# Layer 3's attention: float32r scores from two row halves, readings and row sums between the pairs

## Chip, cores and metric

The kernel runs on one core of a Trainium2 chip (trn2). The metric is the device time of one execution in microseconds (us), taken as the median of several. Lower is better.

## The reference, cut to what matters

The kernel computes four transformer-like layers on x (64 batches of 64 tokens, 256 features). The change is in the attention of layer 3, eight heads over a context `ctx_2048` of the same shape:

```python
def _L3_xattn_ref(q, k, v, gamma):
    ...
    qh = q.reshape(B, h, dq, Lq)
    kh = k.reshape(B, h, dq, Lk)
    vh = v.reshape(B, h, dv, Lk)
    scale = 1.0 / jnp.sqrt(jnp.asarray(dq, dtype=q.dtype))
    qk = jnp.einsum('bhdq,bhdl->bhql', qh, kh) * scale
    sm = jax.nn.softmax(qk, axis=-1)
    ret = jnp.einsum('bhql,bhdl->bhdq', sm, vh)
    return gamma * ret.reshape(B, Dv, Lq)
x = x + _L3_xattn_ref(_layernorm(x, axis=-1), ctx_2048, ctx_2048, L3_xattn_gamma)
```

The 64 tokens of a batch play the part of the channels: a head has 8 of them, and the 256 features are the positions. So there are 64 x 8 score matrices of 256 x 256, each a product over only 8 channels, in float32 accuracy.

## The kernel before, in words

**Tiles, quads, units.** Two batches make a tile of 128 rows; there are 32 tiles. A tile has 16 (batch, head) pairs, called units, in four quads i of four units r. Tiles run in order, written out for the first and last four and as a loop over groups of four between.

**Operands.** Products in float32 accuracy are made from bfloat16 parts. The context, as keys, is split into three parts by GpSimd (POOL) in layer 0's attention (`split`, L355 to L359) and stored to `k_parts` in device memory. The normalized x, as queries, is split into three parts during layer 3's attention, four tiles ahead (`AHEAD`): VectorE (DVE) normalizes (L230), ScalarE (ACT) copies the high part (`high`, L2807) and the middle one (`mid`, L2814), POOL makes the rest and the low part (`rest_and_low`, L2678, L2682). SyncE (SP) stores them (`store`, L2590), waits until they have landed, and loads q and k for four tiles ahead of the one just finished (`load`, L2598, L2601, L2605): 9 products of parts x 8 channels = 72 rows (`ROWS3`), 4 KB per row and batch. The first four tiles are loaded in the stage before (ternary). Rows 72 and 73 of q hold the negated row maxima, against ones in k.

**Two passes of scores.** For each unit TensorE (PE) first makes the scores with queries on partitions (`score`, L2722: two matmuls, 72 rows, 256 columns), two tiles ahead (`LEAD`). DVE takes their maxima, negated (`maxima`, L2855). POOL splits the 128 x 32 maxima of a tile in two bfloat16 parts (`split_max`, L2658, L2660), PE transposes them (`turn_max`, L2733), ACT copies them to `rows` (`rows_copy`, L2800), and SP lays them into rows 72 and 73 of q (`lay_rows`, L2612). In the second pass PE makes the scores turned, keys on partitions, with 74 rows, so that the maximum is already taken off (`score_turned`, L2742), and ACT takes the exponential (`exponent`, L2825).

**Reading.** `read` multiplies a quad's exponentials with the values (L2759) and with ones, for the row sums (L2765). Each matmul there uses a strip of 32 columns of the array, four strips side by side; float32 matmuls run as two instructions, so the records count twice as many as the code. For the quads in `SUMMED` (0 to 2) POOL has added up the two halves of the keys before (`add_lengths`, L2668), and the row sums take 4 matmuls, otherwise 8. ACT copies the tile's output and row sums away (`out_copy`, L2819, L2820), DVE inverts the sums (L2861), POOL multiplies and adds to x (`finish`, L2689, L2691).

**Order.** Each engine's order is written out by hand. PE, per quad i of tile a: for r in 0 to 3 a score of tile a+2 and a turned score of tile a; then the reading of quad i-1. The transpose for tile a+1 stands before quad 2. ACT: four exponentials per quad; the output copies of tile a-1 stand behind exponential (1, 0), the rows' copy before quad 2, `high` behind (2, 3), `mid` behind quad 3. POOL: `split_max` in quad 0, values in quad 1, `finish` of tile a-1 behind (2, 3), `rest_and_low` in quad 3. DVE: the reciprocal behind maximum (2, 0). SP, per tile: rows, stores, loads.

**Banks.** Scores use banks 0 to 3, one per unit; turned scores banks 4, 5, 7 and again 4, so that unit 3 must wait for the exponential of unit 0 of its quad and unit 0 for that of unit 3 of the quad before (`turned_after`); the output is in bank 6; the transposed maxima in bank 3.

```python
turned_bank, turned_after = (4, 5, 7, 4), (1, 4, 4, 3)
...
pe.wait_ge(s["exp_ready"], unit_ready(a.t, i, r) - turned_after[r])
...
if i == 0:
    pe.wait_ge(s["val_ready"], tile_ready(a.t))
    pe.wait_ge(s["out_copied"], tile_ready(a.t) - 1)
```

The last wait holds the first reading of a tile until the output of the tile before is copied out.

## Time and profile before

| what | value |
|---|---|
| median of 3 executions | 2258.29 us (2255.62 to 2261.69) |
| the profiled execution | 2276.26 us |
| its span in the trace | 2274.0 us |
| PE, weight loads, DVE, ACT, POOL busy over the span | 84%, 64%, 70%, 44%, 49% |
| layer 3's attention, first score to last reading | about 1420 to 1908 us |
| granted clock of PE in 1460 to 1880 | 1.00 |

The profile is of one execution. Busy shares are over all stages, and a stage has its own limit. Matmuls are pipelined, and the ends of their records are modelled, so what PE spends on one is read from the distance between starts, not from its duration. A number behind an arrow in brackets in a row is idle time of the engine before it, and what ended it.

### The profile page before, as it was taken

Reading aid. Unit: us, or ns where it says so; the run is one execution under the profiler, and the core shown is the slowest. Engines: PE = TensorE matmul, PEld = TensorE weight load, DVE = VectorE, ACT = ScalarE, POOL = GpSimd, SP = SyncE. Lnnn points to the kernel's source line nnn. Section 1 sums busy time; section 2 is a strip of 40 time slices with the busy share of each in tenths; the row PEclk is TensorE's granted clock in tenths of the full one; section 3 lists DMA queues with packets and bytes.
Section 4 is the critical chain, followed back from the end, with each engine's and each line's share of the span. In section 5 each row is a group of like instructions: output and inputs, shape, how many; then the busy total and the mean of one; then the engine's idle time right before and its main releaser. Section 6 shows DMA issues by size and latency. Waiting matters only on the chain. (4 is left out here: it accounts for less than half of the span.)

```text
span 2274.0 us, 46815 instructions
## 1 busy us (share of the span) xinstructions
PE 1915.3 (84%) x15870; PEld 1457.1 (64%) x15870; DVE 1592.3 (70%) x3825; ACT 995.0 (44%) x2486; POOL 1115.9 (49%) x1467
## 2 busy tenths in 40 slices
PE   6979845398885988898887897899999998879993
PEld 5869612387664777777776787466666664547772
DVE  7865732469668889898886665888888785443446
ACT  3733221134233455554443332466666665423330
POOL 4630026524365666666663100488888775643331
PEclk8989857699997999999998999799999999989996
DMA  7631036600240000000000210144444433223337
GB/s 211 230 102 54 10 117 175 186 20 6 63 128 26 1 0 0 0 0 0 0 0 11 69 39 1 31 109 109 109 108 109 106 86 88 88 94 96 106 108 238
DMA packets 140384, 172.62 MB, mean 76 GB/s; under 512 B 31410, under 2 KB 121698, under 8 KB 135586
## 3 DMA queue, kind: packets, MB, share of 16 engines
q1 hardware_dynamic: 130385, 148.01, 23.7%
q0 software_dynamic: 9808, 22.23, 3.3%
q8 instruction: 101, 1.65, 0.3%
q14 instruction: 90, 0.73, 0.1%
HBM read 117.59 MB, written 52.00 MB: 75 GB/s over the span
## 5 line engine op out<-in xcount | busy, mean ns | idle before, releaser
L2855 DVE TENSOR_REDUCE mx<-bank 128x2 f32<-128x512 f32 x512 | 321.0, 678 | 77.9 <-PE bank L2722 77.2
L2825 ACT ACTIVATE e<-bank 128x512 f32<-128x512 f32 x512 | 269.1, 606 | 135.3 <-PE bank L2742 135.3
L2668 POOL TENSOR_TENSOR es<-e 128x256 f32<-128x256 f32 x384 | 271.7, 730 | 90.5 <-ACT e L2825 90.0
L1915 POOL TENSOR_TENSOR q_l<-q_l,rot_l 64x512 f32<-64x512 f32 x128 | 162.3, 1268 | 131.0 <-DVE rot_l L2113 131.0
L2722 PE MATMUL bank<-k,q 72*128 72x256 bf16 x1024 | 203.6, 284 | 15.7 <-DMA k<-k_parts 7.5
L2742 PE MATMUL bank<-q,k 74*128 74x256 bf16 x1024 | 195.5, 274 | 5.9 <-DMA q<-rows 3.8
L2759 PE MATMUL bank<-e,val 128*32 128x256 f32 x2048 | 138.8, 388 | 3.1 <-ACT nd L2820 0.7
L2722 PEld LDWEIGHTS bank<-k,q 72*128 72x128 bf16 x1024 | 92.0, 100 | 76.5 <-issue 24.5
L3040 POOL DMA_INDIRECT y<-y,y_row x71 | 69.2, 975 | 128.4 <-DVE y L3315 123.5
L1947 PE MATMUL bank<-qcT,wq_abs 96*128 96x128 f32 x1024 | 127.4, 285 | 0.0
L1947 PEld LDWEIGHTS bank<-qcT,wq_abs 96*128 96x128 f32 x1024 | 121.5, 198 | 2.5
L1972 PE MATMUL bank<-wvo,rd_l 128*128 128x256 f32 x512 | 116.4, 381 | 0.0
L2742 PEld LDWEIGHTS bank<-q,k 74*128 74x128 bf16 x1024 | 97.5, 98 | 29.2 <-DMA q<-rows 8.6
L3300 DVE TENSOR_TENSOR hid<-bank,sig 128x176 f32<-128x176 f32 x103 | 35.0, 340 | 113.8 <-issue 45.0
L3173 ACT ACTIVATE sig<-bank 128x176 f32<-128x176 f32 x103 | 32.7, 318 | 176.2 <-PE bank L3096 152.9
L1984 PE MATMUL bank<-key_l,q_l 128*64 128x64 f32 x2048 | 75.5, 227 | 40.6 <-POOL q_l L1915 40.6
L2043 ACT ACTIVATE sc_l<-sc_l 128x512 f32<-128x512 f32 x64 | 40.4, 631 | 156.7 <-POOL sc_l L1901 156.7
L1972 PEld LDWEIGHTS bank<-wvo,rd_l 128*128 128x128 f32 x512 | 95.3, 191 | 16.4 <-ACT rd_l L2055 0.4
L1984 PEld LDWEIGHTS bank<-key_l,q_l 128*64 128x64 f32 x2048 | 66.2, 140 | 55.9 <-POOL q_l L1915 42.0
L975 POOL DMA_INDIRECT xg<-xn_rows,slot_idx x16 | 16.1, 1008 | 170.0 <-POOLq L555 165.4
L2111 DVE TENSOR_TENSOR q_l<-bank,const_sb 64x512 f32<-64x512 f32 x128 | 88.9, 694 | 14.9 <-PE bank L1947 10.9
L3096 PE MATMUL bank<-w,xT 128*128 x284 | 98.1, 468 | 0.2 <-issue 0.2
(455 smaller groups left out, 5031.4 us busy)
## 6 DMA issues: line engine op xcount, KB each, us to landing
k<-k_parts SPq DMA_DIRECT2D x96, 192.0 KB
q<-q_parts SPq DMA_DIRECT2D x32, 576.0 KB
got<-rows SPq DMA_DIRECT2D x71, 129.0 KB
moe_rows<-zero_a SPq DMA_DIRECT2D x16, 512.0 KB
w<-in_e0w SPq DMA_DIRECT2D x16, 512.0 KB
parts_y<-y SPq DMA_DIRECT2D x32, 256.0 KB
k_parts<-k_parts_a SPq DMA_DIRECT2D x96, 64.0 KB, 2.1
q_parts<-parts SPq DMA_DIRECT2D x96, 64.0 KB, 2.0
```

The source lines that it names most:

```text
L1915: nc.gpsimd.tensor_tensor(q[64:P, j, four(m), :], q[64:P, j, four(m), :], rot[64:P, j, four(m), :], ALU.add).then_inc(s["rope_added"], 1)
L1947: last = nc.tensor.matmul(bank(j, h // 4)[:, (h % 4) * P:(h % 4 + 1) * P], wq[:, h, :], qcT[:, j, :], start=True, stop=True)
L1972: last = nc.tensor.matmul(bank(j, 2)[:, 0:D], rd[:, j, hp, :], wvo[:, hp, :], start=(hp == 0), stop=(hp == HP - 1))
L1984: last = nc.tensor.matmul(bank(j, h // 8)[r, (h % 8) * S:(h % 8 + 1) * S], q[:, j, h, r], key[:, j, r], start=True, stop=True)
L2111: v.tensor_tensor(q[64:P, j, four(m), :], raw[64:P], tab(c.cos, 64, P), ALU.mult)
L2668: nc.gpsimd.tensor_tensor(es[:, n, :], e[:, n, 0, :], e[:, n, 1, :], ALU.add).then_inc(s["sum_ready"], 1)
L2722: last = nc.tensor.matmul(scores(r)[:, qt * D:(qt + 1) * D], q[0:R, b, h * D + qt * P:h * D + qt * P + P], k[0:R, b, h * D:(h + 1) * D], s ...
L2742: last = nc.tensor.matmul(scoresT(r)[:, lt * D:(lt + 1) * D], k[:, b, h * D + lt * P:h * D + lt * P + P], q[:, b, h * D:(h + 1) * D], star ...
L2759: nc.tensor.matmul(readout[32 * r:32 * r + 32, 0:D], val[:, a.n % 2, r, i, lt, :], e[:, slot(i, r), lt, :], start=(i == 0 and lt == 0), st ...
L2825: nc.scalar.activation(e[:, slot(i, r), :, :].rearrange("p k n -> p (k n)"), scoresT(r)[:, :], ACT.Exp).then_inc(s["exp_ready"], 1)
L2855: v.tensor_reduce(mx[:, a.n, 0, at:at + 2], scores(r)[:, :].rearrange("p (a n) -> p a n", a=2), AX.X, ALU.max, negate=True).then_inc(s["ma ...
L3096: last = nc.tensor.matmul(gates(u)[:, 0:2 * HID3], src(k), w(k), start=(k == 0), stop=(k == DK - 1))
```

## The change

The parts become two float32r ones (a rounded high part and the rest) instead of three bfloat16 ones, for keys and queries: 4 products x 8 channels = 32 rows per head (`ROWS3`). Heads are put in two halves of the partitions, 0 to 63 and 64 to 127 (`BASE3`): units r = 0 and 2 in one, 1 and 3 in the other. Within a half, rows 32 to 61 are zero in q and one in k and stay so, and rows 62 and 63 hold the negated maxima against ones; the first pass uses 62 rows, the second all 64. PE issues units in pairs (`score_pair`, `turned_pair`), alternating between the halves, each into its own bank. Per quad it now issues turned pair 0, score pair 0, the reading (`read`), turned pair 1, score pair 1, the row sums (`read_lengths`). POOL adds up the keys for quads 0 and 1 only. The transposed maxima go to bank 7. The middle parts and their copies are gone (`mid`), `x_low` is one subtraction on POOL that waits for ACT's `high`. q and k of a tile come by four DMAs each instead of one and three, the rows by two.

```diff
 HH3 = HID3 // 2
-BUF3, ROWS3 = 4, 9 * DQ3
+BUF3, ROWS3 = 4, 4 * DQ3
+BASE3, TOP_ROW3 = (0, P // 2), P // 2 - 2
...
             def split(t):
-                parts, rest, src = k_parts[:, t % KR, :, :], k_rest[:, t % KR, :], ctx_in[:, t % CTX, :]
+                parts, src = k_parts[:, t % KR, :, :], ctx_in[:, t % CTX, :]
                 pool.wait_ge(s[ctx_loaded[t % CTX]], 32 * (t // CTX) + 32)
-                wait(pool, k_stored[t % KR], 48 * (t // KR))
-                nc.gpsimd.tensor_copy(parts[:, 0, :], upper(src))
-                nc.gpsimd.tensor_tensor(rest, src, upper(src), ALU.subtract).then_inc(s["a_split"], 1)
+                wait(pool, k_stored[t % KR], 32 * (t // KR))
+                nc.gpsimd.tensor_copy(parts[:, 0, :], src).then_inc(s["a_split"], 1)
                 pool.wait_ge(s["a_split"], t + 1)
-                nc.gpsimd.tensor_copy(parts[:, 1, :], upper(rest))
-                nc.gpsimd.tensor_tensor(parts[:, 2, :], rest, upper(rest), ALU.subtract).then_inc(s["k_low_ready"], 1)
...
+                for n, (a, value) in enumerate(((c.k3, 1.0), (c.q3, 0.0))):
+                    for m, base in enumerate(BASE3):
+                        at = slice(base + ROWS3, base + 2 * ROWS3)
+                        nc.gpsimd.memset(whole(a[at, t, :]), value).then_inc(s["p_keys"], 1)
+                        pool.wait_ge(s["p_keys"], 4 * t + 2 * n + m + 1)
 
             def step(t, j):
                 pool.wait_ge(s["xlow_ready"], ready(t))
                 if t < 2 * BUF3:
-                    nc.gpsimd.memset(c.k3[64:ROWS3 + 2, t, :].bitcast(F32), ONES).then_inc(s["p_keys"], 1)
...
+def head_rows(ap, both, g):
+
+    return ap[:, :, 2 * H3 * both:2 * H3 * both + 2 * H3, :].rearrange("a c (b g h) l -> g (a c) b (h l)", b=2, g=2)[g]
+
+
+def copied_rows(ap, both, g, b):
+
+    return head_rows(ap, both, g)[:, b, :].unsqueeze(1).broadcast_to([2 * DQ3, 2, H3 // 2 * D])
...
-        SUMMED = range(0, QU - 1)
+        SUMMED = range(0, QU - 2)
...
-        max_rows = c.bank[3][0:8 * H3, 0:P]
+        max_rows = c.bank[7][0:8 * H3, 0:P]
...
-                cols, both = bass.ds(2 * a.t * H3, 2 * H3), slice(2 * a.n, 2 * a.n + 2)
-                q_rows = c.q_parts[:, :, cols, :].rearrange("a c h l -> (a c) (h l)").unsqueeze(1)
-                sp.dma_start(q[0:R, both, :], q_rows.broadcast_to([3 * DQ3, 3, 2 * H3 * D])).then_inc(s[qk_loaded[a.n]], 16)
-                k_rows = c.k_parts[:, :, cols, :].rearrange("c m h l -> (c m) (h l)")
-                for m in range(3):
-                    sp.dma_start(k[3 * DQ3 * m:3 * DQ3 * (m + 1), both, :], k_rows).then_inc(s[qk_loaded[a.n]], 16)
+                both = slice(2 * a.n, 2 * a.n + 2)
+                for g, base in enumerate(BASE3):
+                    for b in range(2):
+                        sp.dma_start(whole(q[base:base + R, 2 * a.n + b, :]),
+                                     copied_rows(c.q_parts, a.t, g, b)).then_inc(s[qk_loaded[a.n]], 16)
+                    for m in range(2):
+                        sp.dma_start(whole(k[base + 2 * DQ3 * m:base + 2 * DQ3 * (m + 1), both, :]),
...
-                sp.dma_start(q[R:R + 2, 2 * a.n:2 * a.n + 2, :], rows[:, a.n, :]).then_inc(s[rows_loaded[a.n]], 16)
+                for g, base in enumerate(BASE3):
+                    at = slice(base + TOP_ROW3, base + TOP_ROW3 + 2)
+                    sp.dma_start(whole(q[at, 2 * a.n:2 * a.n + 2, :]),
+                                 whole(rows[4 * H3 * g:4 * H3 * g + 4 * H3, a.n, :])).then_inc(s[rows_loaded[a.n]], 16)
...
+            def x_low(a):
                 b = a.n % 2
-                wait(pool, "xq_ready", a.t + 1)
-                wait(pool, "mid_ready", a.t - 1)
-                wait(pool, "low_ready", a.t)
+                wait(pool, "high_ready", a.t + 1)
                 if a.exists(-2):
-                    pool.wait_ge(s[stored[b]], 48 * uses(a))
+                    pool.wait_ge(s[stored[b]], 32 * uses(a))
                 settle(pool, s["pool_passed"])
-                nc.gpsimd.tensor_tensor(rest[:, b, :], xq[:, b, :], upper(xq[:, b, :]),
-                                        ALU.subtract).then_inc(s["rest_ready"], 1)
-                wait(pool, "rest_ready", a.t + 1)
-                settle(pool, s["pool_passed"])
-                nc.gpsimd.tensor_tensor(parts[:, b, 2, :], rest[:, b, :], upper(rest[:, b, :]),
+                nc.gpsimd.tensor_tensor(parts[:, b, 1, :], xq[:, b, :], whole(parts[:, b, 0, :]),
                                         ALU.subtract).then_inc(s["low_ready"], 1)
...
-            def score(a, i, r, turned=None):
-                if i == 0 and r == 0:
-                    pe.wait_ge(s[qk_loaded[a.n]], 64 * a.g + 64)
-                pe.wait_ge(s["max_ready"], unit_ready(a.t, i, r) - NP1)
-                if turned is not None:
-                    pe.wait_ge(s["rows_ready"], tile_ready(turned.t))
-                b, h = batch_head(a.n, i, r)
+            def score_pair(a, i, p):
+                if i == 0 and p == 0:
+                    pe.wait_ge(s[qk_loaded[a.n]], 128 * a.g + 128)
+                pe.wait_ge(s["max_ready"], unit_ready(a.t, i, 2 * p + 1) - NP1)
                 for qt in range(2):
-                    last = nc.tensor.matmul(scores(r)[:, qt * D:(qt + 1) * D],
-                                            q[0:R, b, h * D + qt * P:h * D + qt * P + P],
-                                            k[0:R, b, h * D:(h + 1) * D], start=True, stop=True)
-                last.then_inc(s["scores_ready"], 1)
-
-            def turn_max(a):
-                if a.exists(1):
-                    pe.wait_ge(s["max_ready"], unit_ready(a.t + 1, 1, 3))
+                    for r in (2 * p, 2 * p + 1):
+                        base, b, at = place(a.n, i, r)
+                        last = nc.tensor.matmul(scores(r)[:, qt * D:(qt + 1) * D],
+                                                q[base:base + TOP_ROW3, b, at + qt * P:at + qt * P + P],
+                                                k[base:base + TOP_ROW3, b, at:at + D], start=True, stop=True)
+                        if qt == 1:
+                            last.then_inc(s["scores_ready"], 1)
+
+            def turn_max(a, freed_at):
+                pe.wait_ge(s["exp_ready"], freed_at)
...
-            def score_turned(a, i, r):
-                if i == 0 and r == 0:
-                    pe.wait_ge(s[rows_loaded[a.n]], 16 * a.g + 16)
-                pe.wait_ge(s["exp_ready"], unit_ready(a.t, i, r) - turned_after[r])
-                b, h = batch_head(a.n, i, r)
+            def turned_pair(a, i, p):
+                if i == 0 and p == 0:
+                    pe.wait_ge(s[rows_loaded[a.n]], 32 * a.g + 32)
+                pe.wait_ge(s["exp_ready"], max(unit_ready(a.t, i, r) - turned_after[r] for r in (2 * p, 2 * p + 1)))
                 for lt in range(DK):
-                    last = nc.tensor.matmul(scoresT(r)[:, lt * D:(lt + 1) * D],
-                                            k[:, b, h * D + lt * P:h * D + lt * P + P],
-                                            q[:, b, h * D:(h + 1) * D], start=True, stop=True)
-                last.then_inc(s["turned_ready"], 1)
+                    for r in (2 * p, 2 * p + 1):
+                        base, b, at = place(a.n, i, r)
+                        used = slice(base, base + TOP_ROW3 + 2)
+                        last = nc.tensor.matmul(scoresT(r)[:, lt * D:(lt + 1) * D], k[used, b, at + lt * P:at + lt * P + P],
+                                                q[used, b, at:at + D], start=True, stop=True)
+                        if lt == DK - 1:
+                            last.then_inc(s["turned_ready"], 1)
 
             def read(a, i):
 
-
-                if i in SUMMED:
-                    pe.wait_ge(s["sum_ready"], 4 * (len(SUMMED) * a.t + i + 1) + 16)
-                else:
-                    pe.wait_ge(s["exp_ready"], unit_ready(a.t, i, 3))
+                pe.wait_ge(s["exp_ready"], unit_ready(a.t, i, 3))
...
+            def read_lengths(a, i):
+
+                if i in SUMMED:
+                    pe.wait_ge(s["sum_ready"], 4 * (len(SUMMED) * a.t + i + 1) + 16)
...
                     turning = i == 2 and a.exists(1)
                     if turning:
-                        turn_max(a.to(1))
-                    for r in range(4):
+                        turn_max(a.to(1), unit_ready(a.t, 1, 2))
+                    for p, part in enumerate((read, read_lengths)):
+                        if turning and p == 1:
+                            pe.wait_ge(s["rows_ready"], tile_ready(a.t + 1))
+                        turned_pair(a, i, p)
                         if a.exists(LEAD):
-                            score(a.to(LEAD), i, r, a.to(1) if turning and r == 3 else None)
-                        score_turned(a, i, r)
-                    if i > 0:
-                        read(a, i - 1)
-                    elif a.exists(-1):
-                        read(a.to(-1), QU - 1)
+                            score_pair(a.to(LEAD), i, p)
+                        if i > 0:
+                            part(a, i - 1)
+                        elif a.exists(-1):
+                            part(a.to(-1), QU - 1)
```

`mid` and the middle part are taken out of ACT's program in the same way here and in the ternary stage, and semaphore counts follow.

PE's order, with the names of the operands (`k,q` a score, `q,k` a turned score, `e,val` a reading, `ones` row sums). Before, quad 3 of the first tile, with the reading of quad 2:

```order
L2722 MATMUL bank<-k,q 128x256 x2
L2742 MATMUL bank<-q,k 128x256 x2
L2722 MATMUL bank<-k,q 128x256 x2
L2742 MATMUL bank<-q,k 128x256 x2
L2722 MATMUL bank<-k,q 128x256 x2
L2742 MATMUL bank<-q,k 128x256 x2
L2722 MATMUL bank<-k,q 128x256 x2
L2742 MATMUL bank<-q,k 128x256 x2
L2759 MATMUL bank<-e,val 32x256 x8
L2765 MATMUL bank<-es,ones 32x256 x4
```

Every score and turned score alternate unit by unit, and the reading with its row sums stands behind all eight pairs of matmuls. The same place with the change:

```order
L2746 MATMUL bank<-q,k 128x256 x4
L2724 MATMUL bank<-k,q 128x256 x4
L2759 MATMUL bank<-e,val 32x256 x8
L2746 MATMUL bank<-q,k 128x256 x4
L2724 MATMUL bank<-k,q 128x256 x4
L2770 MATMUL bank<-e,ones 32x256 x8
```

A reading now stands after the first two turned and the first two scored units, and the row sums after the other two: between one turned pair and the next there are 4 score matmuls and 8 (or 4) narrow ones.

## Rows read from the trace of the kernel before

**Rows 1.** The view of one line, L2733: the transpose, PE.

```profile
L2733 PE MATMUL bank<-const_sb,mx x30: 298/300/300, 1454.2 to 1874.3; 128*64 128x128 f32 x30
```

**Rows 2.** Timeline of PE (start us, us, engine line op operands, count), two quads.

```profile
1650.26 1.05 PE L2765 MATMUL bank<-e,ones 128*32 128x256 f32 x16
1651.23 0.39 PE L2722 MATMUL bank<-k,q 72*128 72x256 bf16 x2
...
1654.82 0.39 PE L2722 MATMUL bank<-k,q 72*128 72x256 bf16 x2
...
1656.37 0.38 PE L2742 MATMUL bank<-q,k 74*128 74x256 bf16 x2
1656.68 1.07 PE L2759 MATMUL bank<-e,val 128*32 128x256 f32 x16
1657.56 0.61 PE L2765 MATMUL bank<-es,ones 128*32 128x256 f32 x8
1658.11 0.39 PE L2722 MATMUL bank<-k,q 72*128 72x256 bf16 x2
```

**Rows 3.** Waits of PE in 1460 to 1880 (us, times, longest).

```profile
PE bank L2722 <- DMA k<-k_parts: 7.5, 11, 1.7
PE bank L2742 <- DMA q<-rows: 3.8, 14, 0.4
```

**Rows 4.** Timeline of PE in the ternary stage: float32r, 256 columns.

```profile
1343.97 0.28 PE L2337 MATMUL bank<-w_t,hhigh_t 128*128 128x256 f32 x1
1344.20 0.28 PE L2337 MATMUL bank<-w_t,hhigh_t 128*128 128x256 f32 x1
```

**Rows 5.** Timeline of weight loads, two 64-column halves in turn, layer 2.

```profile
903.43 1.48 PEld L1984 LDWEIGHTS bank<-key_l,q_l 128*64 128x64 f32 x48 [0.33 <-issue]
```

**Rows 6.** Timeline at the stage's end, where no scores are left.

```profile
1884.72 0.60 ACT L2825 ACTIVATE e<-bank 128x512 f32<-128x512 f32 x1 [1.20 <-PE bank L2742]
...
1885.57 0.37 ACT L2820 COPY nd<-bank 128x256 f32<-128x256 f32 x1
...
1886.09 1.07 PE L2759 MATMUL bank<-e,val 128*32 128x256 f32 x16 [0.33 <-ACT nd L2820]
...
1890.48 0.83 PE L2742 MATMUL bank<-q,k 74*128 74x256 bf16 x6
1890.91 2.07 ACT L2825 ACTIVATE e<-bank 128x512 f32<-128x512 f32 x4 [0.77 <-PE bank L2742]
1891.56 0.11 PEld L2742 LDWEIGHTS bank<-q,k 74*128 74x128 bf16 x2 [0.53 <-ACT e L2825]
```

**Rows 7.** Timeline of DVE in quad 2: the reciprocal and the maxima after it.

```profile
1655.85 1.74 DVE L2861 RECIPROCAL rec<-nd 128x256 f32<-128x256 f32 x1
...
1657.51 4.21 DVE L2855 TENSOR_REDUCE mx<-bank 128x2 f32<-128x512 f32 x7
```

**Rows 8.** The first load's issue, and a window after it (last: DMA share, GB/s).

```profile
1650.37 0.87 SPq L2598 DMA_DIRECT2D q<-q_parts  x1
...
1660.00:1661.00 1.00, 1.00 (x21) 0.65 (x24) 1.00 (x2) 0.83 (x2) 1.00 (x2) 1.00 0.02 5
```

**Rows 9.** Groups of weight loads (count, busy us, mean ns), 1300 to 1908.

```profile
L2742 PEld LDWEIGHTS bank<-q,k 74*128 74x128 bf16 x1024 | 97.5, 98 | 29.2 <-DMA q<-rows 8.6 <-ACT e L2825 5.5 <-issue 1.6
...
L2337 PEld LDWEIGHTS bank<-w_t,hhigh_t 128*128 128x128 f32 x120 | 23.6, 196 | 4.8 <-DVE hlow_t L2442 4.8
```

**Rows 10.** Timeline of PE after the longest wait; windows with busy us, PEclk, DMA.

```profile
1807.10 0.39 PE L2722 MATMUL bank<-k,q 72*128 72x256 bf16 x2 [1.70 <-DMA k<-k_parts]
...
1809.55 1.94 PE L2759 MATMUL bank<-e,val 128*32 128x256 f32 x16
...
1812.81 0.39 PE L2722 MATMUL bank<-k,q 72*128 72x256 bf16 x2
...
1880.00:1900.00 20.00, 17.84 (x232) 9.22 (x224) 5.55 (x7) 14.32 (x30) 15.46 (x26) 1.00 0.01 3
...
1810.00:1820.00 10.00, 9.91 (x116) 5.99 (x109) 6.53 (x10) 5.57 (x13) 7.42 (x15) 0.88 0.58 128
```

More of the change, by code:

```diff
@@ L309, in store @@
                 sp.wait_ge(s["k_low_ready"], t + 1)
-                for a in range(3):
+                for a in range(2):
                     sp.dma_start(c.k_parts[:, a, t * 2 * H3:(t + 1) * 2 * H3, :].rearrange("c h l -> h c l"),
-                                 k_parts[:, t % KR, a, :]).then_inc(s[k_stored[t % KR]], 16)
+                                 whole(k_parts[:, t % KR, a, :])).then_inc(s[k_stored[t % KR]], 16)
             load_x(0)
@@ L344, in _ @@
             for j in range(KR):
-                sp.wait_ge(s[k_stored[j]], 48 * len(range(j, NT, KR)))
+                sp.wait_ge(s[k_stored[j]], 32 * len(range(j, NT, KR)))
             sp.wait_ge(s["zeroed"], 16 * 19)
@@ L2217, in stage_l2_ternary @@
         PARTS = 6
-        ONES = float(np.array([0x3F803F80], np.uint32).view(np.float32)[0])
         p_stored = ("p_stored0", "p_stored1")
@@ L2242, in _ @@
                 both, cols = slice(2 * n, 2 * n + 2), slice(2 * n * H3, 2 * n * H3 + 2 * H3)
-                sp.wait_ge(s["p_mid"], n + 1)
                 sp.wait_ge(s["p_low"], n + 1)
-                for m in range(3):
+                for m in range(2):
                     sp.dma_start(c.q_parts[m, :, cols, :].rearrange("c h l -> h c l"),
-                                 c.parts3[:, n % 2, m, :]).then_inc(s[p_stored[n % 2]], 16)
-                sp.wait_ge(s[p_stored[n % 2]], 48 * (n // 2) + 48)
-                q_rows = c.q_parts[:, :, cols, :].rearrange("a c h l -> (a c) (h l)").unsqueeze(1)
-                sp.dma_start(c.q3[0:ROWS3, both, :],
-                             q_rows.broadcast_to([3 * DQ3, 3, 2 * H3 * D])).then_inc(s["p_loaded"], 16)
+                                 whole(c.parts3[:, n % 2, m, :])).then_inc(s[p_stored[n % 2]], 16)
+                sp.wait_ge(s[p_stored[n % 2]], 32 * (n // 2) + 32)
+                for g, base in enumerate(BASE3):
+                    for b in range(2):
+                        sp.dma_start(whole(c.q3[base:base + ROWS3, 2 * n + b, :]),
+                                     copied_rows(c.q_parts, n, g, b)).then_inc(s["p_loaded"], 16)
             sp.wait_ge(s["m_loaded"], 80)
-            sp.wait_ge(s["p_loaded"], 80 * BUF3)
+            sp.wait_ge(s["p_loaded"], 144 * BUF3)
         @block.gpsimd
@@ L2394, in high @@
                 if n >= 2:
[L2395 to L2400 removed]
+                    act.wait_ge(s[p_stored[n % 2]], 32 * (n // 2))
+                act.copy(c.parts3[:, n % 2, 0, :], c.xq3[:, n % 2, :]).then_inc(s["p_high"], 1)
             def step(t, j):
@@ L2405, in step @@
                 feat_copy(t + 2, j)
-                for lag, job in ((1, high), (2, mid)):
-                    n = part_of(t, lag)
-                    if n is not None:
-                        job(n)
+                n = part_of(t, 1)
+                if n is not None:
+                    high(n)
             def step_before_last(t, j):
@@ L2805, in high @@
                 if a.exists(-2):
[L2806 to L2814 removed]
+                    act.wait_ge(s[stored[b]], 32 * uses(a))
+                act.copy(parts[:, b, 0, :], xq[:, b, :]).then_inc(s["high_ready"], 1)
             def out_copy(a):
@@ L2837, in tile @@
                             high(a.to(AHEAD))
-                    if i == 3 and a.exists(AHEAD):
-                        mid(a.to(AHEAD))
             rows_copy(At(0, 0))
@@ L2863, in norm @@
             def norm(a):
-                wait(dve, "high_ready", a.t - 1)
-                wait(dve, "rest_ready", a.t - 1)
+                wait(dve, "low_ready", a.t - 1)
                 normalize(nc, c, xq[:, a.n % 2, :], a.t).then_inc(s["xq_ready"], 1)
```

114 lines of the change are left out of this document (49 added, 65 removed).

## Prediction

> **What bounds the kernel now.** The change is in one stage, layer 3's attention, so the page's shares over the whole span say little. The first view is that of one line: the transpose of the negated maxima runs once per tile on TensorE (PE), first at 1454.2 and last at 1874.3 in a list of 30 within that window, so a tile takes 420.1 / 29 = 14.49 us [rows 1].
>
> What sets it is read from the timeline of PE over one quad [rows 2]. Sixteen score matmuls run from 1654.82 to 1656.59 without a gap, 0.111 us each (1.77 us). The reading of the previous quad starts 0.09 later and takes 0.88; its row sums take 0.55 to the next score, 0.43 of it streaming and 0.12 the change back to full-width matmuls. Sums of a quad that GpSimd (POOL) has not added up take 0.97 (1650.26 to 1651.23). A quad is 1.77 + 0.09 + 0.88 + 0.55 = 3.29 us, and a tile 4 x 3.29 + 0.42 (one quad's longer sums) + 0.14 (the transpose) + 0.15 (a wait in quad 1) = 13.9: PE never stops. The other 0.6 is waits for loads, of which PE's own records show 7.5 + 3.8 = 11.3 us over 29 tiles, 0.4 per tile [rows 3]. So **PE's work bounds the stage**, and the loads now and then.
>
> **The change, part by part.** (1) *Matmuls.* There are as many as before, 64 per tile, of 256 columns. A float32r matmul of 256 columns follows the one before after 0.118 us (1343.97 to 1344.20 is two) [rows 4]; the bfloat16 one took 0.111. Now two of them use separate halves of the array's rows. No row shows two row halves at work. One end is 0.118 per pair, the other 0.236 (one after the other). I take 0.118, because the nearest row, two 64-column halves of the array, shows weight loads that overlap: 48 loads in 1.48 us start 0.0285 apart, though a single one of 64 columns can't be done in that time if a 128-column one holds the next back for 0.111 [rows 2, 5]. PE's score work falls from 7.1 to 32 x 0.118 = 3.8 us per tile; its readings are as before, and one more quad's sums come unadded (+0.42). PE's work would be some 11 us.
>
> (2) *But the order is new, so the chain of waits has to be walked.* The second order listing shows per quad i: turned pair 0, score pair 0, reading, turned pair 1, score pair 1, row sums. Turned pair 0 writes bank 4, so it waits for the exponential of unit 3 of the quad before; pair 1 writes it again and waits for unit 0 of its own quad. Constants, from the tail of the stage, where ScalarE (ACT) and PE wait for each other [rows 6]: an exponential starts 0.43 after its turned pair (1890.48 to 1890.91); four take 2.07, the last of them 0.60, so they follow each other by 0.49; PE goes on 0.05 after one ends (1891.51 to 1891.56). T is the start of turned pair 0.
>
> Plain quad: pairs until T + 0.47; reading from 0.56; 0.88 + 0.12 later, at 1.56, turned pair 1; exponential 2 at 1.99, exponential 3 from 2.48 to 3.08; next quad at **3.13**. PE itself is ready at 2.03 + 0.09 + 0.55 = 2.67, or 3.09 after unadded sums: level with the chain.
>
> Quad 1: its reading is the first into the output bank, and waits for ACT's two copies of the last tile's output, which stand behind exponential (1,0). The copies end 1.22 after that exponential starts (1884.72 to 1885.94) and the reading starts 0.15 later [rows 6]. Before, PE had 1.77 us of scores ahead of this reading and waited 0.15; now it has 0.47. Reading at 0.43 + 1.22 + 0.15 = 1.80, turned pair 1 at 2.80, exponential 3 from 3.72 to 4.32, next quad at **4.37**: 1.24 us given back in one wait.
>
> Quads 2 and 3: VectorE (DVE) puts the reciprocal between the maxima of units 0 and 1; the next maximum starts 1.66 after it, maxima follow each other by 0.60 [rows 7]. Maximum 0 at 0.67, reciprocal 1.28, maximum 1 from 2.94 to 3.62. Score pair 0 of quad 3 needs it and would be due at 3.13 + 0.24 = 3.37: 0.30 late. So quad 2 is **3.13** and quad 3 **3.43**. The transpose goes in front of quad 2, where PE waits for exponential 3 anyway (done at 4.05 of 4.37), and the copy of its rows fits into ACT's own wait: nothing.
>
> Sum 3.13 + 4.37 + 3.13 + 3.43 = 14.06 us per tile, **0.43 less than 14.49, or 12.5 us over 29 tiles**.
>
> (3) *Loads.* Per tile 1152 KB come in, not 1280 (by the shapes in the code), but by nine DMAs, not five. Now the first is issued at 1650.37, 2.9 us into a tile that starts at 1647.5 (two quads, 7.2, ahead of the transpose before 1654.82), and the last byte lands by 1660 to 1661, 12.5 to 13.5 in [rows 8]; the next tile needs it at 13.9. SP's queue: two stores, not three, released by POOL's one subtraction and no longer by ACT's middle part at the quad's end, so some 1 us earlier; then eight loads of about 0.45 issue instead of four; then the values; the row DMAs are two instead of one, issued some 5 us before use. Since PE's own 14.06 is hardly shorter, the loads have 1 to 2 us more room. Of the 0.4 per tile of waiting, which the 14.06 doesn't contain, I keep 0.1: +2.9 us (bounds 0 and 11.3).
>
> (4) *POOL* adds up 8 units instead of 12 per tile and one subtraction instead of two. It had room; PE waits for its sums only at the quad's end. Nothing. *ACT* loses the copy of the middle part, at the quad's end, off the chain.
>
> (5) *Elsewhere.* In layer 0's attention POOL does two splitting operations instead of four per tile and SP stores 256 KB instead of 192, in 1 KB rows instead of 512 B. In the ternary stage POOL sets 32 blocks of constant rows instead of 8, with nothing waiting before the stage's end some 100 us later. PE fills both stages. Nothing, give or take 2. The two tiles of the lead-in are paced by DVE (0.60 per unit), and two tiles at the end have no scores and are on the same exponential chain: nothing.
>
> Total: -12.5 + 2.9 = **-10 us**. The profiled execution took 2276.3 us (span 2274.0) and would take 2266; it stands 18 us above the median of 2258.3, so I forecast **2248 us**. Error of the walk: 0.1 us per quad is 12 us, and PE is level with the chain in two quads, so this case alone spans 2236 to 2258. A measurement of this kernel tells no more than 0.3% (7 us) from no change.
>
> **Rivals.**
> *A. The halves don't run side by side.* For it: a float32r weight load lasts 196 ns, a bfloat16 one 98 [rows 9], and no row shows row halves. Walk: exponential 0 at 0.55, scores end 0.94, turned pair 1 at 2.03, next quad 3.72 or, with unadded sums, 4.04 by PE; quad 1 4.64; tile 4.04 + 4.64 + 3.72 + 4.04 = 16.4, +1.95 x 29 = +57 and some 3 for the end tiles: **2318**. The Trainium skill (TensorE: Matmul & The Clock Gate, weight-path perf modes and LDWEIGHTS) says that the fast load isn't for float32 types and a load takes columns / 1.2 ns, 107 ns here; 64 one after the other would be 6.8 us. Its part on packing small matmuls says that loads to different row groups overlap and four row tiles gave 3.07 times; by that, A falls. Chance 0.17.
>
> *B. The clock falls.* PE now idles 1.33 us in every quad 1. Before, a wait of 1.70 us was followed 2.5 us later by the low clock: reading and sums took 3.26 us (1809.55 to 1812.81) instead of 1.85 [rows 2, 10]; the granted clock is 0.88 over those 10 us, of 1.00 at 2.4 GHz and 0.50 at 1.2. Against: from 1880 to 1900 PE waits in every quad and the clock stays at 1.00. If it happened in each tile, up to 1.41 x 29 = 41 us on top: **2289**. Chance 0.09.
>
> *C. Changing between row halves and column strips costs more than 0.09 and 0.12.* There are 16 such changes per tile instead of 8, eight of them (around the readings) on the chain. Decided at 0.43 / 8 = 0.05 us more per change: from there on it is slower. If each waited for the 0.27 us of the matmul before, 0.16 more, it is 8 x 0.16 x 29 = +37, to **2285**; at 0.08 more, 2267. The Trainium skill (TensorEngine Tiling, Key Properties) says that changing the tiling mode drains TensorE; by it the larger price is the likelier. The rows show 0.12 for a change from strips to the full array. Chance 0.14.
>
> *D. What PE gains, the waits take exactly* (loads wait as before, or the walk is 0.2 short): within 7 us of 2258. Chance 0.12. *E. More gain:* if the output copies or the reciprocal didn't hold PE, the tile would be 4 x 3.13 = 12.5 and the time 2201; both waits are in the code. Chance 0.03.
>
> **The numbers.** Forecast case 0.45, A 0.17, B 0.09, C 0.14, D 0.12, E 0.03. Faster by over 0.3%: 0.40 of the forecast case and E's 0.03, with 0.05 of the small loads-free end of D: 0.48. Same: 0.05 of the forecast, 0.07 of D, 0.05 of C: 0.17. Slower: A, B and 0.09 of C: 0.35. The range 2232 to 2292 leaves out A and E.
>
> **What would show it.** Right: transposes 14.0 to 14.2 us apart; in each quad 1 PE idle about 1.3 us in front of the reading, put down to ACT's copies; turned pairs whose two units' exponentials start 0.49 apart after one 0.43 delay; waits for k and rows under 3 us in all. Wrong: matmuls of the two halves starting 0.118 apart instead of together and a period over 16 (A); a granted clock under 1.00 in the stage (B); gaps over 0.15 around the readings where nothing is waited for (C).

## The result and the profile after

The changed kernel took 2274.53 us (median of 6 executions, 2271.76 to 2281.43); the kernel before, run beside it, 2257.45 (2255.59 to 2263.22). The ratio is **1.0076, 95% interval 1.0055 to 1.0098: slower by 17 us**, where 2248 us, 10 us faster, was forecast. The profiled execution took 2271.76 us with a span of 2269.8. That is less than the 2276.26 us of the profile before, though the kernel is slower: from its last transpose to its end the profile before took 386.5 us (2274.0 less 1887.5), this one 370.5, and another execution of the kernel before (as_before, below) 367.7. So most of the 18 us by which the profile before stood above its median lie behind the changed stage.

The transpose's line (weight loads; count, ns, first and last start), which answers to [rows 1]:

```profile
L2735 PEld LDWEIGHTS bank<-const_sb,mx x31: 108/108/109, 1450.2 to 1899.3; 128*64 128x64 f32 x31
```

A tile takes (1899.3 - 1450.2) / 30 = 14.97 us. The kernel before has all its 31 transposes from 1454.2 to 1887.5, 14.44 per tile. The 0.53 us more are 16 us over 30 tiles: the stage holds nearly the whole loss.

Who waited in the changed kernel, 1460 to 1880 (us in total, times, longest), where [rows 3] showed loads:

```profile
PEld bank L2746 <- ACT e L2826: 67.4, 140, 0.9
...
PE bank L2759 <- ACT nd L2821: 32.7, 28, 1.2
...
PE bank L2746 <- ACT e L2826: 10.3, 28, 0.4
PEld bank L2724 <- DVE mx L2854: 6.1, 27, 0.2
```

No wait for a load is left; TensorE (PE) now waits for ScalarE (ACT): 1.17 us for the output copies (`nd`) in every tile, near the 1.33 of the forecast, and for exponentials in front of turned pairs. The timeline of one tile from quad 0 on, lines of PE and ACT (start, us, engine, line, operands, count; in brackets idle time and what ended it; here and in the timelines below, weight loads and the engines not spoken of are left out):

```profile
1652.35 0.51 PE L2746 MATMUL bank<-q,k 64*128 64x256 f32 x4
1652.66 0.43 PE L2724 MATMUL bank<-k,q 62*128 62x256 f32 x4
1652.86 1.09 ACT L2826 ACTIVATE e<-bank 128x512 f32<-128x512 f32 x2 [0.65 <-PE bank L2746]
1653.02 1.07 PE L2759 MATMUL bank<-e,val 128*32 128x256 f32 x16
1654.02 0.50 PE L2746 MATMUL bank<-q,k 64*128 64x256 f32 x4
1654.56 1.09 ACT L2826 ACTIVATE e<-bank 128x512 f32<-128x512 f32 x2 [0.61 <-PE bank L2746]
...
1655.70 0.51 PE L2746 MATMUL bank<-q,k 64*128 64x256 f32 x4
1656.24 0.60 ACT L2826 ACTIVATE e<-bank 128x512 f32<-128x512 f32 x1 [0.59 <-PE bank L2746]
1656.73 0.47 ACT L2820 ACTIVATE nd<-bank,gam 128x256 f32<-128x256 f32 x1
1657.09 0.37 ACT L2821 COPY nd<-bank 128x256 f32<-128x256 f32 x1
1657.61 1.07 PE L2759 MATMUL bank<-e,val 128*32 128x256 f32 x16 [1.17 <-ACT nd L2821]
...
1660.28 0.50 PE L2746 MATMUL bank<-q,k 64*128 64x256 f32 x4
1660.62 0.40 PE L2724 MATMUL bank<-k,q 62*128 62x256 f32 x4
...
1663.62 0.50 PE L2746 MATMUL bank<-q,k 64*128 64x256 f32 x4 [0.37 <-ACT e L2826]
...
1667.35 0.39 PE L2746 MATMUL bank<-q,k 64*128 64x256 f32 x2
```

Quads start at 1652.35, 1655.70, 1660.28, 1663.62 and 1667.35: they take 3.35, 4.58, 3.34 and 3.73 us, where 3.13, 4.37, 3.13 and 3.43 were walked. Each is longer than the walk of the prediction had it by 0.21 or 0.22, the last by 0.30. The difference sits behind each turned pair: ACT starts 0.54 later (1654.02 to 1654.56), not 0.43; in quad 2 the score pair starts 0.34 after it (1660.28 to 1660.62), not 0.24. The walk put the reading at T + 0.56 and turned pair 1 at T + 1.56; they start at 0.67 and 1.67. The groups of weight loads (count, busy us, mean ns), 1300 to 1908, name a candidate, against the 98 ns that [rows 9] shows for bfloat16:

```profile
L2724 PEld LDWEIGHTS bank<-k,q 62*128 62x128 f32 x1024 | 83.5, 196 | 25.9 <-DVE mx L2854 21.1 <-POOLq L2648 4.0 <-issue 0.6
L2746 PEld LDWEIGHTS bank<-q,k 64*128 64x128 f32 x1000 | 76.2, 186 | 116.8 <-ACT e L2826 75.6 <-issue 41.1
```

### The profile page after: what moved, and what is told of

The parts are those of the page before. It is cut to its first block and busy times, and to the rows that moved or that the text cites. A ratio compares the mean times of both kernels' runs of the same rounds, so it can differ in the third digit from the quotient of the medians.

```text
span 2269.8 us, 46910 instructions
## 1 busy us (share of the span) xinstructions
PE 1875.2 (83%) x16123; PEld 1402.6 (62%) x16126; DVE 1606.8 (71%) x3825; ACT 993.9 (44%) x2454; POOL 1008.8 (44%) x1267
## 5 line engine op out<-in xcount | busy, mean ns | idle before, releaser
L2826 ACT ACTIVATE e<-bank 128x512 f32<-128x512 f32 x512 | 282.1, 597 | 177.2 <-PE bank L2746 177.2
L2677 POOL TENSOR_TENSOR es<-e 128x256 f32<-128x256 f32 x256 | 183.8, 734 | 149.2 <-ACT e L2826 146.4
L2746 PEld LDWEIGHTS bank<-q,k 64*128 64x128 f32 x1024 | 78.0, 186 | 120.8 <-ACT e L2826 79.2
L2746 PE MATMUL bank<-q,k 64*128 64x256 f32 x1024 | 129.9, 331 | 18.8 <-ACT e L2826 14.1
L2724 PE MATMUL bank<-k,q 62*128 62x256 f32 x1024 | 112.9, 299 | 15.6 <-DVE mx L2854 11.2
L2759 PEld LDWEIGHTS bank<-e,val 128*32 128x32 f32 x2048 | 56.1, 109 | 76.4 <-ACT e L2826 42.7
L2724 PEld LDWEIGHTS bank<-k,q 62*128 62x128 f32 x1024 | 83.5, 196 | 25.9 <-DVE mx L2854 21.1
```

Of the source, the lines that this page charges most:

```text
L2677: nc.gpsimd.tensor_tensor(es[:, n, :], e[:, n, 0, :], e[:, n, 1, :], ALU.add).then_inc(s["sum_ready"], 1)
L2724: last = nc.tensor.matmul(scores(r)[:, qt * D:(qt + 1) * D], q[base:base + TOP_ROW3, b, at + qt * P:at + qt * P + P], k[base:base + TOP_RO ...
L2746: last = nc.tensor.matmul(scoresT(r)[:, lt * D:(lt + 1) * D], k[used, b, at + lt * P:at + lt * P + P], q[used, b, at:at + D], start=True, ...
L2759: nc.tensor.matmul(readout[32 * r:32 * r + 32, 0:D], val[:, a.n % 2, r, i, lt, :], e[:, slot(i, r), lt, :], start=(i == 0 and lt == 0), st ...
L2826: nc.scalar.activation(e[:, slot(i, r), :, :].rearrange("p k n -> p (k n)"), scoresT(r)[:, :], ACT.Exp).then_inc(s["exp_ready"], 1)
```

## The experiments

**Theory 1:** at the head of a group of matmuls, where nothing runs that could hide it, the float32r weight load (186 to 196 ns, not 98) delays the pair and whatever follows, some 0.1 us each time. **Theory 2:** the wait for the output copies comes with the new order, is real, and is worth about what the walk gave it. **Rivals:** changes between row halves and strips (C), the split reading as such, the unadded sums, loads. Each kernel ran beside the kernel before on one chip; that one's median was 2281.5, 2258.0 and 2280.5 us on the three occasions, so only ratios are compared. "Tile" is the first to the last of the transposes' 31 weight loads, divided by 30.

| run | tile, us | ratio to before [95%] |
|---|---|---|
| as_before | 14.38 | 1.0000 [0.9975, 1.0025] |
| as_changed | 15.00 | 1.0088 [1.0060, 1.0116] |
| upper_halves | 14.35 | 0.9987 [0.9967, 1.0006] |
| outcopy_early | 14.06 | 0.9960 [0.9935, 0.9985] |
| both_terms | 13.55 | 0.9873 [0.9851, 0.9894] |
| before_outcopy | 14.53 | 1.0015 [0.9998, 1.0032] |
| one_reading | 14.49 | 0.9996 [0.9976, 1.0016] |
| sum3 | 15.01 | 1.0098 [1.0067, 1.0129] |
| before_sum2 | 14.36 | 0.9973 [0.9957, 0.9990] |
| scores_between | 14.04 | 0.9965 [0.9951, 0.9979] |
| outcopy_recip | 13.78 | 0.9934 [0.9917, 0.9952] |
| between_recip | 13.58 | 0.9888 [0.9868, 0.9908] |

**The two kernels again, unchanged** (as_before, as_changed), one after the other on one chip.

> The kernel before, unchanged, profiled beside the others on one chip. In before_sum2 one more quad's unadded sums did not lengthen the tile (14.36 us between transposes against 14.44 in the profile before). If the kernel before is held by its loads (theory: POOL frees the parts later, the loads start later), its tiles here take 14.4 to 15.0 us with 0.5 or more of waiting for k and rows each; if TensorE's work bounds it, 13.9 to 14.0 and less than in before_sum2.

> The changed kernel, unchanged, beside the others on one chip. Both theories: 1.0076 of the kernel before as on record, within its interval; transposes 14.97 us apart, no wait for loads.

The profiled spans are 2251.1 and 2273.6 us, 22.5 apart. Of these, 30 x 0.62 = 18.7 lie between the first and the last transpose, 1.9 before and 1.9 behind. The early stages' edits cost nothing that could be seen beyond that. as_before also bears on what bounds the kernel before: its tile of 14.38 is nearer to the 14.4 expected of one held now and then by its loads than to the 13.9 to 14.0 of one bounded by PE's work alone, and PE waited 6.1 us for k and 2.8 for the rows in 1460 to 1880.

**Operands as upper halves** (upper_halves): the matmuls read the bfloat16 upper half of each float32r word, so the low bits are left out of the scores; everything else is the changed kernel.

```diff
-  nc.tensor.matmul(scoresT(r)[...], k[used, b, ...], q[used, b, at:at + D], ...)
+  nc.tensor.matmul(scoresT(r)[...], upper(k[used, b, ...]), upper(q[used, b, at:at + D]), ...)
```

The score matmuls are changed in the same way.

> The changed kernel whose score and turned-score matmuls read only the upper 16 bits of each operand as bfloat16, every second half-word; the low bits of the parts are left out of the products. Rows, banks, order and waits are the same; only the type, and with it the weight load (196 ns for float32r, 98 for bfloat16 in the ternary and attention stages before the change), differ. Theory 1 (the walk came out 0.93 us per tile short because the weight load at the head of each group of matmuls stands open, 0.1 us longer in float32r, twice per quad): tile 14.2 instead of 15.0, -24 us, to about 2250; exponentials start 0.43 to 0.45 after their turned pair instead of 0.54. Rival (the missing 0.93 is the price of 16 changes between row halves and strips): 0, 2274.

Timeline of this run, quads 2 and 3 (PE, ACT and DVE):

```profile
1655.74 0.71 DVE L231 TENSOR_SCALAR xq<-x_all,mean_all,rstd_all 128x256 f32<-128x256 f32 x1
...
1656.04 0.40 PE L2746 MATMUL bank<-q,k 64*128 64x256 bf16 x4
1656.28 0.39 PE L2724 MATMUL bank<-k,q 62*128 62x256 bf16 x4
1656.37 1.28 DVE L2854 TENSOR_REDUCE mx<-bank 128x2 f32<-128x512 f32 x2
1656.47 1.09 ACT L2826 ACTIVATE e<-bank 128x512 f32<-128x512 f32 x2 [0.27 <-PE bank L2746]
1656.60 1.07 PE L2759 MATMUL bank<-e,val 128*32 128x256 f32 x16
1657.57 1.74 DVE L2860 RECIPROCAL rec<-nd 128x256 f32<-128x256 f32 x1
1657.60 0.40 PE L2746 MATMUL bank<-q,k 64*128 64x256 bf16 x4
...
1659.18 0.40 PE L2746 MATMUL bank<-q,k 64*128 64x256 bf16 x4 [0.37 <-ACT e L2826]
...
1659.91 0.40 PE L2724 MATMUL bank<-k,q 62*128 62x256 bf16 x4 [0.33 <-DVE mx L2854]
...
1661.81 1.07 PE L2770 MATMUL bank<-e,ones 128*32 128x256 f32 x16
1662.91 0.41 PE L2746 MATMUL bank<-q,k 64*128 64x256 bf16 x4
```

and its weight loads, 1300 to 1908:

```profile
L2724 PEld LDWEIGHTS bank<-k,q 62*128 62x128 bf16 x1024 | 48.0, 95 | 48.7 <-DVE mx L2854 37.4 <-POOLq L2648 4.0 <-issue 0.9
```

The exponential is back at 0.43, the score pair at 0.24, the reading at 0.56, turned pair 1 at 1.56: the walked numbers. Quads 0 to 2 take 3.15, 4.38 and 3.14, as walked. The number that changed with them is a weight load's length, 95 ns for 186 to 196. The single records of both traces, which the views merge, put the whole difference at the head of the group. In 213 (changed kernel) and 222 (this run) turned pairs with a score pair right behind them, the first matmuls of the two halves start 3 ns apart in both kernels (medians, here and in what follows); the next two start 222 ns behind them with float32r operands and 125 with bfloat16, and the weight loads for them 108 ns and 15 ns behind the first ones. The score pair then follows after 118 and 113 ns. So what was lost lies between the first and the second load of a group; why the second float32r load starts so late, no run here shows.

Quad 3 takes 3.73 where 3.43 was walked: its score pair starts 0.73 after the turned pair, 0.49 late and not 0.30. VectorE (DVE) shows why: the two maxima at 1656.37 begin with the last one of quad 1, delayed by the normalization (1655.74), so the reciprocal starts 1.53 into quad 2, not 1.28. That normalization takes 0.70 to 0.71 here and in the changed kernel, but 0.40 in the kernel before; with 0.40, I estimate from these starts, the reciprocal would have been at the walked 1.28. The rest of the 0.30 is at the quad's end, where PE and not the chain ends last: from the unadded row sums to the next tile's first turned pair it takes 1.10 (1661.81 to 1662.91), and the walk had 0.97.

**Copies one exponential earlier** (outcopy_early, on ACT), and the same edit in the kernel before (before_outcopy) and together with the upper halves (both_terms, which leaves the same bits out):

```diff
-                        if (i, r) == (1, 0) and a.exists(-1):
+                        if (i, r) == (0, 3) and a.exists(-1):
                             out_copy(a.to(-1))
```

> The changed kernel with one edit on ScalarE: the two output copies stand behind exponential (0, 3) instead of (1, 0). Theory 1 (the chain of waits, walked with the durations of the changed kernel's trace): in quad 1 the copies start 0.1 us after the quad does and end at 0.95, the reading starts at 1.10 instead of 1.91, exponential 3 ends at 3.73, and the quad takes 3.78 instead of 4.58: 0.8 x 30 tiles = -24 us, to about 2250. Rival (the changes between row halves and column strips are what the stage lost): the wait is only moved, TensorE stays at the same period, 0 to -5 us.

> The kernel before with the output copies one exponential earlier. Theory: the wait for the copies comes from the change, which moved the reading of quad 1 ahead of the second turned pair; before, no wait of TensorE for the copies shows. So nothing: 14.4 us per tile, within 3 us of the kernel before. Rival: the position of the copies was bad for both kernels, and this one gains 5 us or more.

> The changed kernel with both suspected terms taken out together: both operands of the score and the turned matmuls read as the upper bf16 halves of the float32r words (the low bits are left out of the scores, so it computes a coarser softmax), and the output copies one exponential earlier on ScalarE. If the two terms are separate and add up (float32r weight loads 0.62 us per tile, by the run that took them alone; copies 0.91 us per tile, by the run that moved them alone), the transposes come 14.97 - 0.62 - 0.91 = 13.44 us apart and the time is 30 x 1.0 = 30 us below the kernel before. Rival: the two hide behind one another, since both delay the same reading of quad 1, or VectorE, whose reciprocal already holds quad 3 up in both runs, takes the gain: 13.8 us or more per tile and 20 us or less below.

Timeline of outcopy_early, quad 1:

```profile
1660.60 0.50 PE L2746 MATMUL bank<-q,k 64*128 64x256 f32 x4
1660.73 0.47 ACT L2820 ACTIVATE nd<-bank,gam 128x256 f32<-128x256 f32 x1 [0.18 <-PE bank L2770]
...
1661.61 1.07 PE L2759 MATMUL bank<-e,val 128*32 128x256 f32 x16 [0.27 <-ACT nd L2821]
...
1664.28 0.50 PE L2746 MATMUL bank<-q,k 64*128 64x256 f32 x4
```

Quad 1 takes 3.68 instead of 4.58, and the loss becomes a gain of 0.4% (9 us). In the kernel before there was next to nothing to win. Its reading of quad 1 starts 0.31 behind the last turned score now and 0.46 before, which is the 0.15 of waiting that the prediction had. But its ACT now waits for the row sums, and PE, in front of the transpose, for a maximum, which it didn't before; the tile is 0.15 longer than as_before's:

```profile
1651.83 0.48 ACT L2819 ACTIVATE nd<-bank,gam 128x256 f32<-128x256 f32 x1 [1.15 <-PE bank L2765]
```

```profile
PE bank L2733 <- DVE mx L2855: 10.8, 27, 0.4
```

The maximum comes late behind the same normalization, which takes 0.785 in this run and 0.404 in the kernel before (medians of 27). Where it is short it starts while GpSimd stands idle, where it is long GpSimd is adding; whether that is the reason was not tested.

Both terms together give 13.55 where their sum gave 13.44: they add up, less 0.11. The ratio 0.9873 is 29 us, where 30 was expected.

**The rest of the new order:** one_reading (the whole reading behind both pairs, as before the change), sum3 (row sums of three quads on GpSimd again) and before_sum2 (the kernel before with two).

```diff
-                    for p, part in enumerate((read, read_lengths)):
+                    for p in range(2):
...
+                    for part in (read, read_lengths):
```

```diff
-        SUMMED = range(0, QU - 2)
+        SUMMED = range(0, QU - 1)
```

> The changed kernel with the reading and the row sums of a quad together again, behind both pairs (turned, score, turned, score, reading, sums). Theory 1 (walk with the trace's durations): turned pair 1 waits for exponential 0 until 1.19; scores end at 1.76, the reading starts at 1.86, the next quad at 3.29 or, with unadded sums, 3.71; in quad 1 the copies are done by 1.91, so only 0.05 is waited. Tile 3.71 + 3.34 + 3.29 + 3.71 + 0.14 (transpose) = 14.2 instead of 15.0: -24 us, to about 2250. Rival (row halves give nothing at all, the time is in PE's work): between 0 and -6 us, from 8 changes of mode fewer at 0.02 each.

> The changed kernel with GpSimd adding up three quads again, as before. Theory 1 (the exponential chain and PE are level in the quads with unadded sums): only quad 3 shrinks, by under 0.1 us: 0 to -3 us against the changed kernel. Rival (TensorE's work bounds the changed stage): -0.42 per tile, -13 us.

> The kernel before with one part of the change alone: GpSimd adds up two quads instead of three. Its TensorE never stops in this stage, so one more quad's sums cost 0.42 us per tile in full: +13 us, to about 2271. If POOL's additions held TensorE somewhere, it would be less, down to +8.

one_reading missed its 14.2: it took 14.49. Quad 0 is as expected, 3.72 for 3.71 (1652.41 to 1656.13, below), but quads 1 to 3 take 3.57, 3.38 and 3.83, each 0.09 to 0.12 more than expected, which stays unexplained. Quad 0, and the wait in front of turned pairs in 1460 to 1880:

```profile
1652.41 0.50 PE L2746 MATMUL bank<-q,k 64*128 64x256 f32 x4
1652.75 0.40 PE L2724 MATMUL bank<-k,q 62*128 62x256 f32 x4
1653.60 0.50 PE L2746 MATMUL bank<-q,k 64*128 64x256 f32 x4 [0.45 <-ACT e L2827]
...
1654.26 1.07 PE L2759 MATMUL bank<-e,val 128*32 128x256 f32 x16
...
1656.13 0.51 PE L2746 MATMUL bank<-q,k 64*128 64x256 f32 x4
```

```profile
PE bank L2746 <- ACT e L2827: 51.7, 116, 0.5
```

Turned pair 1 waits for exponential 0 with nothing long to do meanwhile (1.19 after pair 0), and the readings then stand behind it on PE. So the split reading fills a wait, and that it also exposed the copies is its price: with the copies moved (outcopy_early, 14.06) it is 0.43 per tile better than the whole reading, without (15.00) 0.51 worse. sum3 took 0.42 us of PE's work out of a tile and won nothing; PE waits that much longer for exponentials (23.2 us in 56 waits, 10.3 in 28 in the changed kernel):

```profile
PE bank L2746 <- ACT e L2826: 23.2, 56, 0.5
```

before_sum2 was expected to cost the kernel before 13 us, since PE bounds it, and was 6 us faster instead; its tile of 14.36 is level with the 14.38 and 14.44 of the kernel before, so the sums cost nothing in the stage and where the 6 us come from isn't shown. The waits of its weight loads for k, 1460 to 1880, against 15.9 us in the kernel before:

```profile
PEld bank L2722 <- DMA k<-k_parts: 1.8, 4, 0.5
```

The likely reading: 0.42 us of sums more, and the loads' waits, about as much (PE's own go from 11.3 us to 0.8, 0.36 per tile), gone. That they go because GpSimd has its parts ready sooner is argued, not shown.

**Scores behind turned pair 0** (scores_between): both score pairs between the two turned pairs, the whole reading behind, three quads summed on GpSimd. In between_recip the reciprocal moves behind the last maximum of quad 1; outcopy_recip is outcopy_early with the reciprocal behind that quad's second maximum.

```diff
-                        if a.exists(LEAD):
-                            score_pair(a.to(LEAD), i, p)
+                        if p == 0 and a.exists(LEAD):
+                            score_pair(a.to(LEAD), i, 0)
+                            score_pair(a.to(LEAD), i, 1)
```

```diff
-                        if (i, r) == (2, 0) and a.exists(-1):
+                        if (i, r) == (1, 3) and a.exists(-1):
                             invert(a.to(-1))
```

> Changed order on the changed data layout, a candidate for a faster kernel: per quad turned pair 0, score pair 0, score pair 1, turned pair 1, then reading and row sums together; three quads added up by GpSimd. Theory 1: both score pairs fill the wait for exponential 0 (over at 1.19), turned pair 1 at 1.19 to 1.53, reading from 1.63, next quad at 3.06, or 3.48 with unadded sums; quad 1 waits for the output copies until 1.91 and has the transpose behind it: 3.48. Tile 3.48 + 3.48 + 3.06 + 3.06 = 13.1 us, up to 13.5 if maxima come late: -45 to -56 us against the changed kernel and -30 or more against the kernel before. Rival (row halves give nothing): no faster than the kernel before.

> The version with both score pairs between the turned pairs, with VectorE's reciprocal of the last tile put behind the last maximum of quad 1 instead of behind the first of quad 2. In the version without this, TensorE waited 0.28 + 0.69 us for maxima in quad 3 (3.87 us against 3.15 for quad 2), because 1.74 us of reciprocal stand ahead of quad 2's last three maxima. Theory: 0.7 us of it goes, 14.04 - 0.7 = 13.3 us per tile, some 20 us less than that version, 28 to 30 us below the kernel before. Rival: the wait only moves to quad 2, since the same 1.74 us stand ahead of quad 1's or quad 2's maxima there: 14.0 us per tile, about 9 us below the kernel before.

> The changed kernel with the output copies one exponential earlier, and the reciprocal behind the second maximum of quad 1, where VectorE sat idle for 1.62 us. Quad 3 took 3.70 us against 3.34 for quad 2 in the changed kernel, with TensorE's score weights waiting 0.23 us for a maximum. Theory: that 0.33 us of quad 3 is the reciprocal's, and it goes: 14.06 - 0.33 = 13.73 us per tile, about 10 us less than with the copies alone, 19 us below the kernel before. Rival: the wait for maxima moves to quad 2, and the time is that of the copies alone, 9 us below.

scores_between, quads 2 and 3, and then quads 2 and 3 of between_recip:

```profile
1661.45 0.50 PE L2746 MATMUL bank<-q,k 64*128 64x256 f32 x4
...
1662.83 1.74 DVE L2862 RECIPROCAL rec<-nd 128x256 f32<-128x256 f32 x1
...
1664.49 4.21 DVE L2856 TENSOR_REDUCE mx<-bank 128x2 f32<-128x512 f32 x7
1664.59 0.50 PE L2746 MATMUL bank<-q,k 64*128 64x256 f32 x4
...
1666.36 0.50 PE L2724 MATMUL bank<-k,q 62*128 62x256 f32 x4 [0.69 <-DVE mx L2856]
...
1668.46 0.51 PE L2746 MATMUL bank<-q,k 64*128 64x256 f32 x4
```

```profile
1656.54 0.50 PE L2746 MATMUL bank<-q,k 64*128 64x256 f32 x4
...
1656.71 1.74 DVE L2862 RECIPROCAL rec<-nd 128x256 f32<-128x256 f32 x1
...
1658.37 4.80 DVE L2856 TENSOR_REDUCE mx<-bank 128x2 f32<-128x512 f32 x8
...
1660.84 0.50 PE L2724 MATMUL bank<-k,q 62*128 62x256 f32 x4 [0.41 <-DVE mx L2856]
```

The first gained 0.35%, 8 us, where 30 or more was expected: of quad 3's 3.87 us (1664.59 to 1668.46), 0.69 is idle for a maximum behind the reciprocal. With the reciprocal starting 0.2 us into quad 2 (1656.54 to 1656.71) instead of 1.4 (1661.45 to 1662.83), the tile falls by 0.46 to 13.58, not to the expected 13.3, as 0.41 us of waiting for a maximum is left. **between_recip is 1.1% (25 us) faster than the kernel before** and computes all that it does. outcopy_recip gains 0.28 per tile over outcopy_early (0.33 expected).

## Why the prediction was wrong, point by point

- **The step that failed is the constants of the walk**, "an exponential starts 0.43 after its turned pair", and with it "reading from 0.56". They were taken from [rows 6], where the operands are bfloat16. With float32r they are 0.54 and 0.67; the 0.1 us is lost twice on the quad's chain, at the head of either turned pair, 0.21 us per quad. [Rows 9] had the 196 against 98 ns, and I used them only for rival A. With bfloat16 operands and nothing else changed the tile falls by 0.65 us (15.00 to 14.35), 19 of the 27 us between -10 and +17, and the records put the difference between the first and the second weight load of a group. The Trainium skill (TensorE: Matmul & The Clock Gate, weight-path perf modes and LDWEIGHTS) says that the fast weight load is on only where the input type isn't FP32; the trace agrees in that 128 columns of float32r take 186 and 196 ns against 95 of bfloat16. Its length for a load of 128 columns, 107 ns by columns / 1.2, is not what the trace shows for float32r, and the measurement decides.
- **The second, smaller one:** "Maximum 0 at 0.67, reciprocal 1.28". DVE still had the normalization (0.70, and not the 0.40 of the kernel before) and quad 1's last maximum ahead of it; reciprocal 1.53. With the constants right, quad 3 still takes 3.73, not 3.43: 0.30 per tile, 9 us. Of this, 0.19 is the score pair's and the rest the 1.10 behind unadded row sums, walked as 0.97. The late maximum hides the constants' error in that quad, which takes 3.73 with either operands, so the two add up: 0.64 in quads 0 to 2 and 0.30 in quad 3 are the 0.94 between 14.06 and 15.00, 28 us over 30 tiles. The 2.9 us for loads that didn't come, and a tile before of 14.44 and not 14.49, make the 27 of it.
- **Quad 1's wait** was right: 4.37 walked, 4.38 with the constants right, 4.58 with the float32r ones. It is the largest single item: moving the copies takes 0.94 off the tile. With this wait in it the walk had only 0.43 per tile of gain to lose, so 0.1 at each of two heads in quads 0 to 2, 0.64 in all, was enough to change the sign. The error given, "0.1 us per quad", was too small by half, as the two heads of a quad err in the same direction.
- **Matmuls side by side (A)** was right to be thought unlikely: the first matmuls of the two halves start 3 ns apart, and from a pair to the next group it takes 0.31 to 0.34 us (1652.35 to 1652.66), 0.24 in bfloat16, where one after another would take 4 x 0.118 = 0.47.
- **C** fell: worked out from the starts, the gaps around the readings are 0.10 (0.33 from score pair to reading less 2 x 0.118) and 0.12 (1.00 from reading to turned pair less 0.88), about as before, for twice as many changes. The Trainium skill (TensorEngine Tiling (Array Packing), Key Properties) has a change of tiling mode drain TensorE. Whether it drains, the trace doesn't show, but a change costs no more than these 0.12.
- **B** fell: the granted clock was 1.00 from 1460 to 1900, with 1.17 us idle in every tile:

```profile
1860.00:1900.00 40.00, 34.69 (x468) 18.92 (x459) 28.68 (x43) 25.64 (x52) 22.31 (x40) 1.00 0.19 39
```

- **D** didn't come: the loads' waits went to none, better than the +2.9 us I left. **E**'s two waits were real, and worth moving: outcopy_early, between_recip and outcopy_recip show it. (By the forecast's own sum E's time would be 2248 less 1.54 x 29, 2203 and not 2201.)

## What to carry to other kernels

When a change leaves PE's work and puts a chain of handovers in its place, the chain's constants must be read from rows with the same operand types: a tenth of a microsecond at each of two handovers per quad was more than the whole gain. List what a removed cover was hiding (here 1.77 us of scores ahead of a wait for copies) and move the exposed instruction on its own engine in the same change. An operation of 1.74 us on an engine that feeds the others is best put where the others need nothing from it for a while; its place was worth 0.46 us of 14 here (scores_between to between_recip).

## What the runs showed of the hardware

- A float32r weight load of 128 columns takes 186 to 196 ns, a bfloat16 one 95 to 98, in row halves as in the full array. Inside a run of matmuls it hardly shows (steps of 118 ns against 113); at the head of a group the second matmul of a half starts 222 ns behind the first, against 125, and the exponential behind the pair comes 0.1 us later.
- Two row halves with float32r operands work side by side: their first matmuls start 3 ns apart, and a pair of four takes 0.085 us per matmul of 256 columns including the head, 0.060 in bfloat16, against 0.118 and 0.111 one after another.
- The same normalization on VectorE took 0.40 us in the kernel before, 0.70 in the changed one and 0.785 in before_outcopy. What GpSimd does at that moment differs between them; the cause was not tested.
- Taking 0.42 us per tile of work off TensorE where it waits in a chain gave nothing (sum3). Giving it 0.42 us more where it bounds the stage left the tile as it was in one run (before_sum2), with the waits for loads gone.
